# Graph attention in one kernel: head sums of the drops turned and added on VectorE, place one-hots built once on ScalarE's queue

## The reference

```python
hs = (x @ Ws + bs).reshape(N, H, HD)          # H = 8 heads of HD = 96
hd = (x @ Wd + bd).reshape(N, H, HD)
hs_e = hs[src]
e = leaky_relu(hs_e + hd[dst], 0.2)
logits = einsum('ehd,hd->eh', e, attn)
m = segment_max(logits, dst)
ex = exp(logits - m[dst])
alpha = ex / segment_sum(ex, dst)[dst]
out = elu(segment_sum(alpha[..., None] * hs_e, dst)).reshape(N, DM)
h = layer_norm(out + h, ln_w[l], ln_b[l])     # and this twice
```

## Time and profile before

| what | value |
|---|---|
| median of 3 runs | 2149.63 us (2147.95 to 2150.61) |
| profiled execution: time, span | 2149.37 us, 2147.3 us |
| PE, PEld busy | 2057.0 us (96%), 1669.1 us (78%) |
| DVE, ACT busy | 1652.7 us (77%), 1160.0 us (54%) |
| POOL busy | 975.0 us (45%) |
| DMA | 427.41 MB, mean 199 GB/s |
| granted clock of TensorE, mean | 0.984 |

### The profile page before, as it was taken

How to read it: one execution, slowest core, us unless ns; L and a number is a source line. 1 busy time by engine, 2 the same in 40 slices (tenths; PEclk the granted TensorE clock), 3 DMA queues, 4 the chain that set the end, 5 groups by cost and what they waited for, 6 DMA issues and landing times. The chain is left out here.

```text
span 2147.3 us, 85544 instructions
## 1 busy us (share of the span) xinstructions
PE 2057.0 (96%) x29551; PEld 1669.1 (78%) x29552; DVE 1652.7 (77%) x3737; ACT 1160.0 (54%) x3113; POOL 975.0 (45%) x1023
## 2 busy tenths in 40 slices
PE   7999999998899999999998899899999999999798
PEld 4665555555799999999997555589999999999676
DVE  5545882564699999999998764489999999999884
ACT  2101200014677777777775423477777777777584
POOL 0000010120577777777773211267777777777020
PEclk9999999999999999999999999999999999999899
DMA  6000233995788888888884224488888888888411
GB/s 202 1 0 8 82 106 122 261 277 148 226 269 270 264 276 271 270 267 277 270 271 140 90 88 135 126 252 271 271 270 269 272 262 279 272 267 271 182 58 50
DMA packets 191648, 427.41 MB, mean 199 GB/s; under 512 B 60291, under 2 KB 128841, under 8 KB 191537
## 3 DMA queue, kind: packets, MB, share of 16 engines
q0 software_dynamic: 59584, 298.64, 44.8%
q1 hardware_dynamic: 128155, 119.85, 18.3%
q10 hardware_dynamic: 3828, 7.85, 1.1%
HBM read 385.68 MB, written 29.10 MB: 193 GB/s over the span
## 5 line engine op out<-in xcount | busy, mean ns | idle before, releaser
L531 ACT ACTIVATE at_relu<-at_turned,ah_attn_size 128x512 f32<-128x512 f32 x1092 | 713.4, 687 | 308.5 <-PE at_turned L605 298.2
L507 POOL DMA_INDIRECT at_rows<-table,ah_index x360 | 425.0, 1180 | 176.2 <-POOL ah_index L495 72.0
L507 POOL DMA_INDIRECT ah_room<-table,ah_index x352 | 422.1, 1199 | 167.9 <-POOL ah_index L495 65.8
L711 DVE SCALAR_TENSOR_TENSOR at_relu<-at_relu,ah_pair_sign 128x512 f32<-128x512 f32 x546 | 377.1, 744 | 9.4 <-ACT at_relu L531 9.3
L741 DVE SCALAR_TENSOR_TENSOR sums<-sums,at_factor,at_total 128x97 f32 x1456 | 358.5, 307 | 4.5 <-PE at_total L647 1.1
L601 PE MATMUL at_turned<-ident,ah_room 128*128 128x128 f32 x2208 | 341.7, 278 | 19.0 <-PEq L1701 19.0
L601 PE MATMUL at_turned<-ident,at_rows 128*128 128x128 f32 x2160 | 331.0, 276 | 0.1
L601 PEld LDWEIGHTS at_turned<-ident,ah_room 128*128 128x128 f32 x2208 | 243.9, 142 | 39.9 <-issue 39.8
L601 PEld LDWEIGHTS at_turned<-ident,at_rows 128*128 128x128 f32 x2160 | 236.3, 141 | 19.9 <-issue 19.9
L731 DVE TENSOR_TENSOR at_spread<-at_lined,at_weight 128x1024 f32<-128x1024 bf16 x182 | 221.4, 1217 | 4.1 <-ACT at_weight L542 4.1
L605 PE MATMUL at_turned<-ah_place,dst_rows 96*128 96x128 bf16 x2208 | 216.0, 220 | 0.0
(11 more groups left out here) (315 smaller groups left out, 2904.2 us busy)
## 6 DMA issues: line engine op xcount, KB each, us to landing
at_flags<-run_flags SPq DMA_DIRECT2D x182, 64.0 KB
dst_rows<-pr_parts SPq DMA_DIRECT2D x76, 144.0 KB, 2.7
ah_place<-places SPq DMA_DIRECT2D x92, 96.0 KB
dst_rows<-local_rows SPq DMA_DIRECT2D x13, 672.0 KB, 4.9
places<-dst_rows SPq DMA_DIRECT2D x13, 672.0 KB, 6.8
at_place<-places SPq DMA_DIRECT2D x90, 96.0 KB
table<-ah_room SPq DMA_DIRECT2D x20, 400.0 KB, 4.9
ah_room<-table,ah_index POOLq DMA_INDIRECT x368
```

The source lines that it names most:

```text
L507: pool.indirect_dma_start(rows[b][:, j, :], None, table, bass.IndirectOffsetOnAxis(index[b][:, j:j + 1], 0)).then_inc(gathered[b], 16)
L531: act.activation(relu[c][:], turned[chunk(b, c)][:], ACT.Relu, scale=attn_size[:, c:c + 1]).then_inc(bent, 1)
L711: dve.scalar_tensor_tensor(relu[c][:], relu[from_][:], pair_sign[:, c:c + 1], relu[c][:], ALU.mult, ALU.add).then_inc(joined, 1)
```

## The change

In `attend`, ACT writes the drop as 128 x 128 (the rise times `head_rows`, no mask of quarters), into the room of `iota_row`. `sum_drops` becomes `turn_drops`: PE turns that block into 128 columns of `at_back` by a transpose. DVE has a new instruction, `fold_drops`, between the first and the second join: it adds four columns to one, for 8 results, out of PSUM into a new SBUF tile `at_fold`, and signals `folded`. `factors` waits for `folded` in place of `turned_back` and reads `at_fold`.

In the first turnover, a batch is up to 4 x 7 groups: each quarter of the partitions holds 7 groups with 32 nodes, once and not three times. There are 4 builds (28, 28, 28 and 7 groups), after `source(1)`, `source(3)`, `source(5)` and `source(7)`, and their `rule` (the lines table) one `source` later. Loads and stores of the batches are on ACT's queue. A load of a macro's places in `attend` and at the end of `turnover` reads each of 32 rows three times, in place of 96 stored rows.

```diff
@@ attend, ACT
-                    act.activation(drop[:], quarter_mask[:, 0], ACT.Relu, scale=rise[:]).then_inc(dropped, 1)
+                    act.activation(drop[:], head_rows[:], ACT.Relu, scale=rise[:]).then_inc(dropped, 1)
...
                 def factors(m, b):
-                    act.wait_ge(turned_back, 2 * m + 2)
+                    act.wait_ge(folded, m + 1)
                     for j in range(G):
-                        act.activation(factor[b % 2][:, j, :], back[:, P + j * HH:P + (j + 1) * HH], ACT.Exp,
+                        act.activation(factor[b % 2][:, j, :], fold[:, j, :], ACT.Exp,
@@ attend, PE
-                    pe.matmul(back[:, P:P + G * HH], head_rows[:], drop[:], start=True, stop=True).then_inc(turned_back, 1)
+                    pe.transpose(back[:, P:2 * P], drop[:], ident[:]).then_inc(turned_back, 1)
@@ attend, DVE
+                def fold_drops(m):
+                    dve.wait_ge(turned_back, 2 * m + 2)
+                    dve.tensor_reduce(fold[:], back[:, P:2 * P].rearrange("p (j k g) -> p j k g", j=G, g=HM)[:, :, 0:HH, :], AX.X, ALU.add).then_inc(folded, 1)
...
                     if head:
-                        for k in range(len(JOINED)):
-                            join(head[0], k)
+                        join(head[0], 0)
+                    if message:
+                        fold_drops(message[0])
+                    if head:
+                        join(head[0], 1)
+                        join(head[0], 2)
@@ attend, SP
-                    sp.dma_start(place[b][:], places[bass.ds(m, 1)].rearrange("o p e -> (o p) e")).then_inc(local_loaded[b], 16)
+                    sp.dma_start(place[b][:], places[bass.ds(m, 1)].rearrange("o n e -> (o n) e").unsqueeze(1).broadcast_to([S, SPLIT, ME])).then_inc(local_loaded[b], 16)
@@ turnover
-BATCHES, BUILT = NM // BATCH, 5
+BATCH, BUILT = 7, 5
+BUILDS = [(at, min(QS, (NM - at) // BATCH)) for at in range(0, NM, QS * BATCH)]
+BUILD_SLOTS = range(1, 2 * len(BUILDS), 2)
@@ turnover, SP
-                        store_many(t)
-                        load_many(t + 2)
...
-                    if layer == 0 and NT + t < BATCHES:
-                        store_many(NT + t)
-                        if NT + t + 2 < BATCHES:
-                            load_many(NT + t + 2)
@@ turnover, ACT
+                    load_many(0)
+                    load_many(1)
+                    for k in range(len(BUILDS)):
+                        store_many(k)
+                        if k + 2 < len(BUILDS):
+                            load_many(k + 2)
+                        store_ruled(k)
@@ turnover, DVE
                     for t in range(NT):
                         source(t)
-                        build(t)
+                        if t in BUILD_SLOTS:
+                            build(BUILD_SLOTS.index(t))
+                        if t - 1 in BUILD_SLOTS:
+                            rule(BUILD_SLOTS.index(t - 1))
```

More of the change, by code:

```diff
@@ L340, in persistent @@
         block_list=dram("block_list", [SLOTS], I32),
-        places=dram("places", [NM, SP_ROWS, ME], BF16),
+        places=dram("places", [NM, S, ME], BF16),
         lines=dram("lines", [NM, P, G * S], BF16),
@@ L422, in attend @@
         right, shifted = sb("at_right", [P, P]), sb("at_shifted", [P, P])
-        drop = sb("at_drop", [P, G * HH])
+        drop, fold = iota_row, sb("at_fold", [P, G, HH])
         weight = sb("at_weight", [P, G * H])
@@ L680, in slot @@
                     if head:
-                        sum_drops(head[0])
+                        turn_drops(head[0])
                     if turn:
@@ L1654, in heads_half, with turnover @@
     return ap.rearrange("p (g x) -> p g x", x=H * QUAD)[:, :, half * H * QUAD // 2:(half + 1) * H * QUAD // 2]
-def turnover(layer, ahead, Wsrc, bsrc, Wdst, bdst, attn, ln_w, ln_b, sums, dst_rows, worn, index_ready, local_loaded, gathered, nc, ident, iota_row, split_of, local_rows, dst_local, places, lines, nodes, table, head_mask,
+def turnover(layer, ahead, Wsrc, bsrc, Wdst, bdst, attn, ln_w, ln_b, sums, dst_rows, worn, index_ready, local_loaded, gathered, nc, ident, iota_row, node_of, local_rows, dst_local, places, lines, nodes, table, head_mask,
              src_index, run_flags, global_rows, **_):
@@ L1786, in _ @@
                     load_w(w_dst, Wdst, dst_w_loaded)
-                    load_many(0)
-                    load_many(1)
                     for t in range(NT):
                         store(t)
-                        store_many(t)
-                        load_many(t + 2)
-                    sp.wait_ge(many_stored[0], 16)
+                    for b in range(2):
+                        sp.wait_ge(many_stored[b], 16 * sum(groups for _, groups in BUILDS[b::2]))
                 sp.wait_ge(fresh, 1)
                 for b in range(2):
-                    sp.dma_start(ahead.place[b][:], places[b]).then_inc(local_loaded[b], 16)
+                    sp.dma_start(ahead.place[b][:], places[b].unsqueeze(1).broadcast_to([S, SPLIT, ME])).then_inc(local_loaded[b], 16)
                 for t in range(NT):
@@ L1828, in split, with load_many, store_many, store_ruled @@
                             act.activation(heads_half(parts[t % 2][:, s, :], half), heads_half(dst_row[:], half), ACT.Copy).then_inc(split_done, 1)
+                def load_many(k):
+                    at, groups = BUILDS[k]
+                    if k > 1:
+                        act.wait_ge(many_stored[k % 2], 16 * QS)
+                    act.dma_start(many[k % 2][0:groups * S], local_rows[at:at + groups * BATCH].rearrange("(q m) j e -> q (m j e)", q=groups)
+                                  .unsqueeze(1).broadcast_to([groups, S, BATCH * ME])).then_inc(many_loaded[k % 2], 16)
+                def store_many(k):
+                    at, groups = BUILDS[k]
+                    act.wait_ge(many_made, k + 1)
+                    for q in range(groups):
+                        first = at + q * BATCH
+                        act.dma_start(places[first:first + BATCH].rearrange("m p e -> p m e"),
+                                      many[k % 2][q * S:(q + 1) * S].rearrange("p (m e) -> p m e", m=BATCH)).then_inc(many_stored[k % 2], 16)
+                def store_ruled(k):
+                    at, groups = BUILDS[k]
+                    act.wait_ge(ruled_made, k + 1)
+                    act.dma_start(lines[at:at + groups * BATCH].rearrange("m p e -> p m e"),
+                                  ruled[k % 2][:, 0:groups * BATCH * G].rearrange("p (m j) d -> p m (j d)", j=G)).then_inc(ruled_stored[k % 2], 16)
                 def scale_attn():
```

47 lines of the change are left out of this document (16 added, 31 removed).

## The result

The changed kernel takes 2171.02 us (median of 4 runs, 2170.00 to 2173.72); the kernel before, on the same chip, takes 2149.91 (4 runs, 2147.95 to 2150.61). The ratio is 1.0105, 95% interval 1.009 to 1.012: slower by 21 us, where 52.9 were forecast. The time lies inside the forecast range of 2160 to 2212, near its lower end, and the sign is the forecast one.

The account below looks back on a forecast made before the run. ACT's loop from the weights to the last bend was taken to bound the slot. Drop 0.10 plus factors 0.22 us, x 178 = 57.0, less 4.1 for the turnover, gave 2202.5 us, 2.5% slower; range for 8 in 10, 2160 to 2212.

Parts of the forecast that it names:

- The loop from the weights to the last bend on ScalarE: Edge passes: ACT runs 3.74 us without a hole up to the bend of c5; anything added there lengthens the slot equally.
- The drop: ACT, edge pass: 128 columns for 8 add 0.10 us a slot between the drop and the bend behind it.
- The pair of turns on PE: PE, edge pass: saves 0.08 to 0.11 us a slot, counted as zero because ACT is last there.
- The fold: DVE, edge pass: takes 0.18 us, pushes the joins by 0.1, covered by DVE's waiting and some 0.2 us slack; counted zero.
- The turnover: First turnover: PE's stop of 4.12 us goes, since no build stands behind `source(8)`; 4.1 us won, 0 at worst.
- B: Rival, ACT: only the drop's columns count, factors stay 0.145 apart, paced by address instructions; 2162 us, chance 0.12.
- C: Rival, DVE: the fold's signal comes too late and becomes the releaser of the factors; 2225 us and up, chance 0.06.
- E: Rival, edge pass: ACT's additions hide at issue, PE's saving becomes a wait, only the turnover gives; 2145.5 us, chance 0.08.
- A: Favoured case: ACT's loop sets the slot, so the drop's and factors' additions count in full; 2188 to 2211 us, chance 0.64.
- PE waits too, though hardly a view says so: Head sums, edge pass: PE's weight loads begin about 0.05 us behind ACT's last bend, so PE waits for ACT.
- rival D: PE is the bound after all and ACT's 1.58 us idle real room, so PE's 0.11 counts; 2125 us, chance 0.10.
- the factors: ACT, edge pass: reading SBUF for PSUM spaces four factors 0.20 us apart for 0.145, adding 0.22 us a slot.

Follow-up runs that it names:

- onehots_alone: Kernel before with only the edits of the first turnover and the place loads, old edge pass kept: 2142.30 us, ratio 0.9979 to the kernel before.
- wide_drop: Kernel before, but ACT writes the drop with 128 columns and the old product takes the first 8: 2154.36 us, ratio 1.0040 to the kernel before.
- late_factors_product: Kernel before with the last bend (c5) moved ahead of the four factors on ACT: 2148.58 us, ratio 0.9997 to the kernel before.
- fold_psum: Changed kernel, but DVE writes its eight sums into PSUM and the factors read them there: 2151.85 us, ratio 1.0018 to the kernel before.
- late_factors: Changed kernel with the last bend (c5) moved ahead of the four factors on ACT: 2140.86 us, ratio 0.9960 to the kernel before.
- fold_later: Changed kernel with the fold moved behind the second join on DVE: 2286.08 us (one run), ratio 1.064 to the kernel before.
- late_loop8: late_factors with TensorE's own loop body of 8 slots in place of 4: 2314.36 us, ratio 1.0764 to the kernel before.

## Why the prediction was right in sign and wrong in size

**Held.** The loop from the weights to the last bend on ScalarE does set the slot with the change (in the 400 us above, TensorE's only wait for another engine is the one for that bend). The drop costs +0.101 us (0.10 predicted). The pair of turns on PE saves 0.115 (0.08 to 0.11), and the slot shows none of it. The fold is covered: 0.18 long, the joins 0.10 later, nothing behind it late. The turnover gives 4.6 us by onehots_alone and 5.3 in the profiled execution (4.1 predicted). B, C and E are each excluded by a run or by rows of the changed kernel: factors 0.186 apart, ScalarE without a hole ahead of them, +26.6 us for the edge part alone. Of the prediction's signs two came out smaller than named: slots of 6.93 for about 7.1, and VectorE's wait at 0.59 for 0.7. Its upper bound for A doesn't follow from its own terms: 0.36 us a slot gives 2209, not 2211.

**The step that failed** is "PE waits too, though hardly a view says so", with its conclusion that "what is added to ACT between the weights and the last bend makes the slot longer by the same". It read the wait off the weight loads, which begin 0.05 us behind ACT's last bend. The array's products started 0.110 us behind the bend, 0.057 later than when they truly wait for it, and stood 0.089 apart throughout. PE and ACT were both at their limit to within 0.06 us, with PE the later. That is the slack of rival D, put there at "0.0 by rows 3 and 4". wide_drop shows it (0.101 added, 0.051 paid), and late_factors_product shows that nothing was to be had on ACT. It is worth 0.057 x 178 = 10 us. D's own outcome, a faster kernel, didn't come: the additions on ACT were larger than the slack.

**The term that was mis-sized** is that of the factors. 0.22 us were taken, from the 0.20 us from one other SBUF activation of the slot to the next. The four measure 0.746 - 0.578 = 0.168, a spacing of 0.186 or 0.187 for 0.144. Worked out from the Trainium skill ("ScalarE: Activation LUTs", the section on what ACT_TABLE_LOAD costs) the estimate for that spacing is 0.188. The Trainium skill's "VectorE: DVE Perf Modes" (the section on the TRN2 errata) puts 52 cycles, by estimate 0.043 us, between PSUM and SBUF: measured 0.042. Both pages were nearer than the rows chosen. Behind SBUF factors the last bend is also 0.048 us shorter (0.680 for 0.728), which no term had; fold_psum shows both go back together. So 0.22 should have been 0.12, 18 us over all slots. The 10 and the 18 us make up most of the 32 by which the forecast was too high.

**The account of a slot**: 0.101 + 0.168 - 0.048 - 0.057 = 0.164 us, measured 0.170 in the median. In the mean it is 0.152, because the slot with the jump (one in four) was already 0.09 us longer before the change and is only 0.02 longer than the others with it. 0.152 x 178 - 5 = 22 us, against 21.1 measured.

## What to carry to other kernels

Where TensorE seems to wait, look at the starts of its products and not at its weight loads: here a group of 24 that was 0.84 us long in all slots but one had not waited, though its loads had. When two engines are both within a few hundredths of the limit, a saving on one gives nothing and a cost on the other is paid only past the gap; measure the gap before multiplying by the number of slots. And where an engine's chain is the loop, put the work that ends the chain (here the last bend) ahead of work that is needed later (the factors). That order turned a change that cost 1% into a gain of 0.4%, half of it the turnover's; in the kernel before, where TensorE set the slot, it gave nothing.

## What the runs showed of the hardware

- A [128, 2] activation with a pointer operand is spaced 0.144 us out of PSUM and 0.186 out of SBUF, with the same address instructions ahead of it in the changed kernel and in fold_psum. A 512-column bend behind four such is 0.728 long after the first kind and 0.680 after the second. Why is open.
- TensorE stops at its loop's jump. From the last product of c5 to the first load of the messages are 0.15 us in other slots. In the one with the jump they are 0.21 to 0.24 in the four kernels with the old product (before, onehots_alone, wide_drop, late_factors_product) and 0.31 to 0.39 in those with the turn (0.31 with the change, 0.37 in late_factors, 0.38 in fold_later). It doesn't follow which engine sets the slot: TensorE does in late_factors_product (0.22), ScalarE in fold_later. What makes the difference is open.
- A loop body of 8 slots is fetched anew at each jump back: 20 stops of 3.5 to 6.8 us in late_loop8. Behind the one shown the granted clock is 0.50 (1.2 GHz) from 993.3 to 996.0, and the 64 messages take 2.89 us for 1.58; the mean granted clock of the execution is 0.960 for 0.984.
